# A sparse graph attention kernel: gathers ahead of the edge-to-row matrix, scale and store behind the second square

## The chip, the cores and the metric

The kernel runs on one core of a Trainium2 chip. The metric is the device time in microseconds (us). TensorE is written PE here, VectorE DVE, ScalarE ACT, GpSimd POOL, and SyncE SP.

## What is computed

There are N = 8192 nodes with 128 features. `adj` is an 8192 x 8192 matrix of int32, 256 MB, nearly all zeros (about two ones in a row). The reference, cut to what matters:

```
h = x @ W
e = (h @ a1)[:, None] + (h @ a2)[None, :]
e = where(e > 0, e, 0.2 * e)
e = where(adj > 0, e, -9e15)
attention = softmax(e, axis=1)
z = elu(attention @ h)
y = layernorm(x + z, axis=-1)
```

## The kernel before

It reads all of `adj`, but finds the few ones of each row and works on these alone. A row tile is 128 rows. A step handles two row tiles, so there are 32 steps, numbered 0 to 31 here, and the adj of a step is loaded in four parts of 2 MB, each half the columns of a row tile. Work is spread over a software pipeline: while step n loads and squares, later phases of steps n-1, n-2 and n-3 (in the code p1, p2, p3), and the output of step n-4 (p4), are done. Steps 0 to 5 are written out, 6 to 30 run (in pairs) in a hardware loop with step 30 written out behind it, and step 31, with what is left of the older ones, is a tail in an order of its own. Two places (`g`) alternate for buffers.

In one step, each engine does this, in program order. The order of each engine's queue is what sets the order of the work; there is no planner.

- SP (L353 to L359): four loads of adj, each as soon as a square has freed its slot.
- ACT (L500 to L516): `square_half` 0 to 3 turn the int32 parts into bf16 and count ones (L464). Between them lie `scale` and `store` of p4 (L486 to L498: two activations of 128 x 128 with `shift` and `rstd`, then the output transfer), `distances` of p1 (L475: distance of each edge position to the middle of a row's edges), `copy_sums` of p3 (L482), `exp_weights` of p2 (L467) and `exp_elu` of p3 (L471).
- PE (L640 to L657): `fold_half` 0 (eight products with powers of two, so that eight columns fall into one number), `count_starts` of p1 (a prefix sum of edges, L589), `sum_neighbours` of p3 (L622: gathered rows `nb` times `spread`, 12 instructions of L627 and 4 of L630), fold 1, `send_scores` of p2 (L603, needs the edge-to-row matrix and the gathered rows' scores), `times_W` of p3, `fill_edges` of p1 (L594, sends each edge its row's data), fold 2, fold 3, `send_shares` of p2.
- DVE (L926 to L949): `pick` 0 (L776: eight largest of the folded row and their places), `route` of p1, `neighbour_scores` of p2 (L863, waits for the gathers), pick 1, `rows_to_edges` of p1 (L832), `scores` of p2, `indices` of p1 (L839: copies `edge_in`, then six small operations until `index` at L859), pick 2, `weights` of p2, `finish` of p3 (L903, ends in `mean_var`), pick 3, `edge_weights` of p2 (L896), `lists` of the step itself (L784, ends in `half_len`).
- POOL (L425 to L434): `edges_to_rows` of p1 (L331 to L337: six comparisons that make `edge_row`, the edge-to-row matrix, from `edge_in`), `gather` of p1 (L414: five indirect transfers of 128 rows of x each, from `index`), `norm_factors` of p3 (L401, `rstd` and `shift`), `spread_weights` of p2 (L393, makes `spread`).

`hold` (L50) is a wait with an increment of a spare semaphore. `gather` waits for `index` and for the sum that last read the place it writes. PE's `sum_neighbours` waits for `spread`; fold 1 is behind it in PE's queue; DVE's pick 1 and `rows_to_edges` wait for fold 1; `fill_edges` waits for these; `indices` waits for `fill_edges`.

Of the kernel before, what the change touches and what calls it, by code (L numbers as in the profile page):

```python
# [49 lines left out]
def hold(eng, sem, value, spare):  # L50

    eng.wait_ge(sem, value)
    eng.sem_inc(spare, 1)


def graph_attention(nc, x, adj, W, a, out):
# [39 lines left out]
    with ExitStack() as stack:  # L96
# [213 lines left out]
        def stage(i, g, k):  # L310
            j, place = i - (k - g + 1) // GROUPS, (g - k) % GROUPS
            return None if isinstance(j, int) and not 0 <= j < BODIES else (j, place)
# [18 lines left out]
        def edges_to_rows(eng, j, g):  # L331

            for t in range(PAIR):
                for k, c in enumerate(SPANS[t]):
                    last_one = eng.tensor_scalar(edge_row[:, g, t, k, :], row_iota[:, t * P:(t + 1) * P],  # L335
                                                 edge_in[:, c, ROW_COL:ROW_COL + 1], None, ALU.is_equal)
            last_one.then_inc(edge_row_made, 1)  # L337

        with nc.Block() as block:
# [39 lines left out]
            @block.gpsimd  # L379
            def _(pool):  # L380
                nc.gpsimd.iota(offset[:], pattern=[[1, P]], base=0, channel_multiplier=-1).then_inc(iotas_ready, 1)
                nc.gpsimd.iota(code_base[:].rearrange("p t h s b -> p (t h) s b"),
                               pattern=[[0, PAIR], [-HALF, 2], [0, 8], [-FOLD, BITS]], base=N,
                               channel_multiplier=0).then_inc(iotas_ready, 1)
                nc.gpsimd.iota(row_id[:], pattern=[[P, TILES]], base=1, channel_multiplier=1).then_inc(iotas_ready, 1)
                nc.gpsimd.iota(edge_iota[:], pattern=[[1, EDGES]], base=0, channel_multiplier=0).then_inc(iotas_ready, 1)
                nc.gpsimd.iota(edge_id[:], pattern=[[P, CHUNKS]], base=0, channel_multiplier=1).then_inc(iotas_ready, 1)
                nc.gpsimd.iota(row_iota[:], pattern=[[1, PAIR * P]], base=1, channel_multiplier=0).then_inc(iotas_ready, 1)
                nc.gpsimd.iota(slot_iota[:], pattern=[[1, SLOTS]], base=0, channel_multiplier=0).then_inc(iotas_ready, 1)

                pool.wait_ge(consts_ready, 1)

                def spread_weights(j, g):  # L393
                    hold(pool, edge_w_ready, count(j, g), pool_spare)
                    for t in range(PAIR):
                        mine = edge_w[:, SPANS[t][0]:SPANS[t][0] + SPAN]
                        last = nc.gpsimd.tensor_tensor(spread[:, t, :, :], edge_row[:, g, t, :, :],  # L397
                                                       mine.unsqueeze(2).to_broadcast([P, SPAN, P]), ALU.mult)
                    last.then_inc(spread_ready, 1)

                def norm_factors(j, g):  # L401

                    hold(pool, stats_ready, count(j, g), pool_spare)
                    if not (first(j) and g == 0):
                        hold(pool, scaled, count(j, g) - 1, pool_spare)
                    pool.sem_clear(p_step)
                    v = Steps(pool, p_step)
                    v.after(nc.gpsimd.tensor_tensor(var_eps[:], mean_var[:, :, 1], eps_all[:], ALU.add))
                    v.after(nc.gpsimd.tensor_tensor(rstd[:], var_eps[:], minus_half[:], ALU.pow))  # L409
                    v.after(nc.gpsimd.tensor_tensor(scaled_mean[:], mean_var[:, :, 0], rstd[:], ALU.mult))  # L410
                    nc.gpsimd.tensor_tensor(shift[:], scaled_mean[:], minus_one[:], ALU.mult  # L411
                                            ).then_inc(norm_ready, 1)

                def gather(j, g):  # L414
                    hold(pool, indexed, count(j, g), pool_spare)
                    if not first(j) and not is_final(j, g):
                        hold(pool, summed, count(j, g) - GROUPS, pool_spare)
                    for c in range(CHUNKS):

                        nc.gpsimd.indirect_dma_start(  # L420
                            out=nb_of(j, g)[:, c, :], out_offset=None, in_=x[:, :],
                            in_offset=bass.IndirectOffsetOnAxis(ap=index[:, g, c:c + 1], axis=0),
                            bounds_check=N - 1, oob_is_err=False).then_inc(gathered[g], 16)

                def step(i, g):  # L425
                    p1, p2, p3 = (stage(i, g, k) for k in (1, 2, 3))
                    if p1:
                        hold(pool, edge_in_ready, count(*p1), pool_spare)
                        edges_to_rows(nc.gpsimd, *p1)
                        gather(*p1)  # L430
                    if p3:
                        norm_factors(*p3)
                    if p2:
                        spread_weights(*p2)  # L434

                steps(pool, step)


                gather(*back1)
                spread_weights(*back2)  # L440
                gather(*final)
                norm_factors(*back3)
                spread_weights(*back1)
                norm_factors(*back2)
                spread_weights(*final)
                norm_factors(*back1)
                norm_factors(*final)

            @block.scalar
            def _(act):  # L450
# [3 lines left out]
                def square_half(i, g, q):  # L454
                    h = g * 2 * PAIR + q
                    act.wait_ge(loaded[h % LOAD_SLOTS], i * (16 * HALVES // LOAD_SLOTS)
                                + 16 * (h // LOAD_SLOTS + 1))
                    if not (first(i) and h < SQUARES):
                        act.wait_ge(folded, i * HALVES + (h + 1 - SQUARES))
                    if first(i) and h == SQUARES - 1:  # L460
                        act.wait_ge(s_ready, 1)
                    if q == 0 and not first(i):
                        act.wait_ge(listed, count(i, g) - GROUPS)
                    nc.scalar.activation(square[:, h % SQUARES, :], adj_sb[:, h % LOAD_SLOTS, :], ACT.Square,  # L464
                                         accum_out=half_sum[:, h:h + 1]).then_inc(squared, 1)

                def exp_weights(j, g):  # L467
                    act.wait_ge(scored, count(j, g))
                    nc.scalar.activation(weight[:], score_e[:], ACT.Exp).then_inc(weighed, 1)  # L469
# [12 lines left out]
                def copy_sums(j, g):  # L482
                    act.wait_ge(summed, count(j, g))
                    nc.scalar.copy(x_att[:], x_att_ps[:, :, 0:P]).then_inc(x_att_ready, 1)

                def scale(j, g):  # L486
                    act.wait_ge(norm_ready, count(j, g))
                    if not first(j):
                        act.wait_ge(out_stored[g], j * 16)
                    for t in range(PAIR):  # L490
                        last = nc.scalar.activation(y_out[:, g, t, :], y[:, t, :], ACT.Identity,  # L491
                                                    bias=shift[:, t:t + 1], scale=rstd[:, t:t + 1])
                    last.then_inc(scaled, 1)

                def store(j, g):
                    act.wait_ge(scaled, count(j, g))
                    nc.scalar.dma_start(out_tiles[:, bass.ds(j * BODY + g * PAIR, PAIR), :],
                                        y_out[:, g, :, :]).then_inc(out_stored[g], 16)  # L498

                def step(i, g):  # L500
                    now, p1, p2, p3, p4 = (stage(i, g, k) for k in range(5))
                    square_half(*now, 0)
                    if p4:
                        scale(*p4)
                        store(*p4)
                    square_half(*now, 1)
                    if p1:
                        distances(*p1)
                    if p3:
                        copy_sums(*p3)  # L510
                    square_half(*now, 2)
                    if p2:
                        exp_weights(*p2)
                    if p3:
                        exp_elu(*p3)
                    square_half(*now, 3)  # L516

                steps(act, step)


# [569 lines left out]
```

## Time and profile before

| | |
|---|---|
| median of 3 runs | 827.56 us (827.25 to 828.65) |
| span of the profiled execution | 828.0 us; no other time is listed for it |
| PE busy | 579.1 us, 70% |
| DVE busy | 597.4 us, 72% |
| ACT busy | 548.5 us, 66% |
| POOL busy | 367.6 us, 44% |
| loads of adj and the other transfers of SP's queue | 272.70 MB, 82.5% of 16 DMA engines |
| mean transfer rate | 345 GB/s |

The span is cut into 40 slices on the page, with the busy share of each engine and the rate of the transfers. The table of waits adds up, by pair, who waited for whom. The chain of waits follows the end of the program back to what released each piece of work. The timeline gives start, duration and, in square brackets, the idle time ahead with its releaser. No engine is busy all the time, so the order and the waits matter more than the sums.

### The profile page before, as it was taken

Reading aid. Unit: us, or ns where it says so; the run is one execution under the profiler, and the core shown is the slowest. Engines: PE = TensorE matmul, PEld = TensorE weight load, DVE = VectorE, ACT = ScalarE, POOL = GpSimd, SP = SyncE. Lnnn points to the kernel's source line nnn. Section 1 sums busy time; section 2 is a strip of 40 time slices with the busy share of each in tenths; the row PEclk is TensorE's granted clock in tenths of the full one; section 3 lists DMA queues with packets and bytes.
Section 4 is the critical chain, followed back from the end, with each engine's and each line's share of the span. In section 5 each row is a group of like instructions: output and inputs, shape, how many; then the busy total and the mean of one; then the engine's idle time right before and its main releaser. Section 6 shows DMA issues by size and latency. Waiting matters only on the chain.

```text
span 828.0 us, 11768 instructions
## 1 busy us (share of the span) xinstructions
PE 579.1 (70%) x3037; PEld 400.7 (48%) x3037; DVE 597.4 (72%) x2487; ACT 548.5 (66%) x482; POOL 367.6 (44%) x543
## 2 busy tenths in 40 slices
PE   6965766776766677676666776766677676667764
PEld 6833444554544445444444554544445454444563
DVE  7366677667777877777777777778777777777862
ACT  0586666786676678766766786676678766769311
POOL 0004455444455544444555444455544444555342
PEclk9988689888888998888889888888998888889976
DMA  8999999999999989999999999999999999998000
GB/s 255 428 428 419 420 417 381 362 351 367 369 361 373 399 353 360 372 359 362 357 406 363 363 364 363 361 363 375 385 370 346 378 361 360 359 403 326 19 20 20
DMA packets 34822, 285.57 MB, mean 345 GB/s; under 512 B 5880, under 2 KB 14224, under 8 KB 18416
## 3 DMA queue, kind: packets, MB, share of 16 engines
q1 hardware_dynamic: 20976, 272.70, 82.5%
q0 software_dynamic: 5120, 8.42, 3.0%
q10 hardware_dynamic: 8704, 4.20, 1.7%
q8 instruction: 9, 0.15, 0.1%
q14 instruction: 13, 0.11, 0.0%
HBM read 283.18 MB, written 4.19 MB: 347 GB/s over the span
## 4 chain that ended last, share of the span: by engine, by line
POOL 29%; PE 27%; issue 21%; DVE 11%; DMA 5%; ACT 4%; SPq 2%; POOLq 1%; ACTq 1%; DVEq 0%
POOL nb L420 14%; PE fold L584 10%; PE x_att_ps L627 8%; POOL edge_row L335 8%; PE small L599 5%; DMA adj_sb<-in_adj 4%; ACT square L464 3%; DVE top_map L780 3%; POOL rstd L409 2%; DVE row_edge L835 2%; POOL spread L397 2%; PE x_att_ps L630 2%; DVE top_col L781 2%; SPq L349 1%; DMA nb<-in_x,index 1%
## 5 line engine op out<-in xcount | busy, mean ns | idle before, releaser
L464 ACT ACTIVATE square<-adj_sb 128x4096 bf16<-128x4096 int32 x128 | 462.0, 3611 | 48.1 <-DMA adj_sb<-in_adj 30.1
L584 PE MATMUL fold<-square,bit_ident 128*128 128x512 bf16 x1024 | 268.7, 411 | 84.5 <-ACT square L464 82.5
L335 POOL TENSOR_SCALAR edge_row<-row_iota,edge_in 128x128 f32<-128x128 int32 x180 | 106.3, 604 | 369.5 <-DVE edge_in L845 369.5
L584 PEld LDWEIGHTS fold<-square,bit_ident 128*128 128x128 bf16 x1024 | 100.0, 107 | 221.6 <-ACT square L464 95.9
L420 POOL DMA_INDIRECT nb<-in_x,index x160 | 166.4, 1040 | 61.1 <-issue 43.7
L780 DVE MAX8 top_map<-fold 128x8 f32<-128x512 f32 x128 | 89.3, 697 | 74.8 <-PE fold L584 74.6
L491 ACT ACTIVATE y_out<-y,shift,rstd 128x128 f32<-128x128 f32 x64 | 28.1, 485 | 143.1 <-POOL shift L411 143.1
L627 PE MATMUL x_att_ps<-spread,nb 128*128 128x128 f32 x384 | 98.9, 430 | 5.8 <-POOL spread L397 3.2
L592 PE MATMUL misc<-found,before 128*128 128x2 f32 x64 | 17.9, 349 | 111.7 <-DVE half_len L816 111.7
L627 PEld LDWEIGHTS x_att_ps<-spread,nb 128*128 128x128 f32 x384 | 87.2, 326 | 9.0 <-POOL spread L397 9.0
L781 DVE FIND_INDEX8 top_col<-top_map,fold 128x8 uint32<-128x512 f32 x128 | 88.4, 690 | 0.0
L866 DVE CUSTOM_DVE_ANT_0 dot<-nb,wa_bc 128x128 f32<-128x128 f32 x160 | 37.8, 296 | 57.1 <-DMA nb<-in_x,index 57.1
L592 PEld LDWEIGHTS misc<-found,before 128*128 128x128 f32 x64 | 15.3, 295 | 127.1 <-DVE half_len L816 127.0
L609 PEld LDWEIGHTS misc<-t_slot,edge_row 128*128 128x128 f32 x384 | 51.1, 204 | 16.1 <-issue 12.0
L599 PE MATMUL small<-sent,row_edge 128*128 128x12 f32 (+1 forms) x384 | 45.9, 254 | 17.2 <-DVE row_edge L835 17.2
L609 PE MATMUL misc<-t_slot,edge_row 128*128 128x10 f32 x384 | 48.7, 261 | 11.0 <-DVE t_slot L870 11.0
L397 POOL TENSOR_TENSOR spread<-edge_row,edge_w 128x384 f32<-128x384 f32 x64 | 51.6, 827 | 7.1 <-DVE edge_w L901 7.1
L599 PEld LDWEIGHTS small<-sent,row_edge 128*128 128x128 f32 (+1 forms) x384 | 41.6, 178 | 25.7 <-DVE row_edge L835 24.1
L618 PEld LDWEIGHTS small<-share,row_edge 128*128 128x128 f32 (+1 forms) x384 | 43.1, 176 | 7.3 <-DVE share L892 1.8
L618 PE MATMUL small<-share,row_edge 128*128 128x10 f32 (+1 forms) x384 | 42.0, 242 | 1.2 <-DVE share L892 1.2
L469 ACT ACTIVATE weight<-score_e 128x20 f32<-128x20 f32 x32 | 7.0, 219 | 49.9 <-DVE score_e L884 49.9
L630 PE MATMUL x_att_ps<-empty_diag,x_mean_bc 128*128 128x128 f32 x128 | 39.9, 414 | 0.0
(106 smaller groups left out, 718.9 us busy)
## 6 DMA issues: line engine op xcount, KB each, us to landing
adj_sb<-in_adj SPq DMA_DIRECT2D x128, 2048.0 KB, 9.7
out<-y_out ACTq DMA_DIRECT2D x32, 128.0 KB, 6.1
nb<-in_x,index POOLq DMA_INDIRECT x160, 7.1
W_sb<-in_L_gnn_W SPq DMA_DIRECT2D x1, 64.0 KB, 1.9
x_sb<-in_x SPq DMA_DIRECT2D x4, 0.5 KB, 9.7
a_sb<-in_L_gnn_a SPq DMA_DIRECT2D x2, 0.5 KB, 2.0
```

The source lines that it names most:

```text
L335: last_one = eng.tensor_scalar(edge_row[:, g, t, k, :], row_iota[:, t * P:(t + 1) * P], edge_in[:, c, ROW_COL:ROW_COL + 1], None, ALU.is_e ...
L397: last = nc.gpsimd.tensor_tensor(spread[:, t, :, :], edge_row[:, g, t, :, :], mine.unsqueeze(2).to_broadcast([P, SPAN, P]), ALU.mult)
L420: nc.gpsimd.indirect_dma_start(out=nb_of(j, g)[:, c, :], out_offset=None, in_=x[:, :], in_offset=bass.IndirectOffsetOnAxis(ap=index[:, g, ...
L464: nc.scalar.activation(square[:, h % SQUARES, :], adj_sb[:, h % LOAD_SLOTS, :], ACT.Square, accum_out=half_sum[:, h:h + 1]).then_inc(squar ...
L584: last = nc.tensor.matmul(fold[:, h % LOAD_SLOTS, :], bit_ident[:, b, :], square[:, h % SQUARES, b * FOLD:(b + 1) * FOLD], start=b == 0, s ...
L599: last = nc.tensor.matmul(edge_in_ps[lo:hi, c, :], row_edge[:, g, t, e:e + hi - lo], sent[:, t, :], start=True, stop=True)
L609: last = nc.tensor.matmul(t_row_ps[:, t, :], edge_row[:, g, t, k, :], t_slot[:, c, :], start=k == 0, stop=k == SPAN - 1)
L618: last = nc.tensor.matmul(share_ps[lo:hi, c, :], row_edge[:, g, t, e:e + hi - lo], share[:, t, :], start=True, stop=True)
L627: nc.tensor.matmul(x_att_ps[:, t, 0:P], nb_of(j, g)[:, c, :], spread[:, t, k, :], start=k == 0, stop=False)
L630: last = nc.tensor.matmul(x_att_ps[:, t, 0:P], x_mean_bc[:], empty_diag[:, t, :], start=False, stop=True)
L780: v.after(nc.vector.max(top_map[:, q, :], fold[:, h % LOAD_SLOTS, :]))
L781: nc.vector.max_index(top_col[:, q, :], top_map[:, q, :], fold[:, h % LOAD_SLOTS, :]).then_inc(picked, 1)
```

## The change

POOL issues the gathers of p1 ahead of the comparisons that make its edge-to-row matrix. ACT does scale and store of p4 not between squares 0 and 1, but behind square 1, `distances` and `copy_sums`, ahead of square 2. The tail is unchanged.

```diff
 # POOL
                 def step(i, g):
                     p1, p2, p3 = (stage(i, g, k) for k in (1, 2, 3))
                     if p1:
+                        gather(*p1)
                         hold(pool, edge_in_ready, count(*p1), pool_spare)
                         edges_to_rows(nc.gpsimd, *p1)
-                        gather(*p1)
                     if p3:
                         norm_factors(*p3)
                     if p2:
 # ACT
                     square_half(*now, 0)
-                    if p4:
-                        scale(*p4)
-                        store(*p4)
                     square_half(*now, 1)
                     if p1:
                         distances(*p1)
                     if p3:
                         copy_sums(*p3)
+                    if p4:
+                        scale(*p4)
+                        store(*p4)
                     square_half(*now, 2)
```

## Rows read from the trace of the kernel before

**Rows 1.** The page, part 2: transfer rate in 40 slices of the span.
```profile
GB/s 255 428 428 419 420 417 381 362 351 367 369 361 373 399 353 360 372 359 362 357 406 363 363 364 363 361 363 375 385 370 346 378 361 360 359 403 326 19 20 20
```

**Rows 2.** Table of waits: engine line waited for, us in total, times, longest.
```profile
POOL edge_row L335 <- DVE edge_in L845: 369.5, 30, 59.1
ACT y_out L491 <- POOL shift L411: 143.1, 29, 5.2
...
DVE dot L866 <- DMA nb<-in_x,index: 57.1, 30, 3.1
...
PEld x_att_ps L627 <- POOL spread L397: 9.0, 28, 1.2
```

**Rows 3.** Chain that ended last, in order of time: start, us, engine, tile.
```profile
551.20 1.65 PE x_att_ps L627 x6
...
561.84 1.08 POOL edge_row L335 x2
```

**Rows 4.** Timeline of PE, one step and the start of the next.
```profile
407.85 1.65 PE L627 MATMUL x_att_ps<-spread,nb 128*128 128x128 f32 x6
...
411.75 2.59 PE L584 MATMUL fold<-square,bit_ident 128*128 128x512 bf16 x8
...
416.64 1.38 PE L599 MATMUL small<-sent,row_edge 128*128 128x12 f32 x12 [0.51 <-DVE row_edge L835]
...
425.30 1.90 PE L584 MATMUL fold<-square,bit_ident 128*128 128x512 bf16 x8 [0.59 <-ACT square L464]
431.18 0.59 PE L592 MATMUL misc<-found,before 128*128 128x2 f32 x2 [3.98 <-DVE half_len L816]
431.86 1.65 PE L627 MATMUL x_att_ps<-spread,nb 128*128 128x128 f32 x6
```

**Rows 5.** Timeline of DVE in the same step.
```profile
418.06 0.22 DVE L845 COPY edge_in<-small 128x60 f32<-128x60 f32 x1 [0.54 <-PE small L599]
...
419.35 0.17 DVE L859 TENSOR_SCALAR index<-edge_code 128x5 uint32<-128x5 f32 x1
...
430.43 0.62 DVE L815 TENSOR_SCALAR to_middle<-found 128x2 f32<-128x2 f32 x1
```

**Rows 6.** Timeline of POOL in the same step.
```profile
418.49 3.54 POOL L335 TENSOR_SCALAR edge_row<-row_iota,edge_in 128x128 f32<-128x128 int32 x6 [10.69 <-DVE edge_in L845]
422.20 1.15 POOL L420 DMA_INDIRECT nb<-in_x,index  x1 [0.17 <-issue]
...
427.59 1.04 POOL L420 DMA_INDIRECT nb<-in_x,index  x1 [0.31 <-issue]
...
430.20 1.61 POOL L397 TENSOR_TENSOR spread<-edge_row,edge_w 128x384 f32<-128x384 f32 x2
```

**Rows 7.** Timeline of ACT in the same step.
```profile
407.92 3.62 ACT L464 ACTIVATE square<-adj_sb 128x4096 bf16<-128x4096 int32 x1 [0.68 <-ACT y_out L491]
...
417.56 0.22 ACT L469 ACTIVATE weight<-score_e 128x20 f32<-128x20 f32 x1 [1.16 <-DVE score_e L884]
```

**Rows 8.** Timeline of DVE and of POOL in the tail: last index, first gather behind it.
```profile
789.20 0.21 DVE L845 COPY edge_in<-small 128x60 f32<-128x60 f32 x1
...
790.39 0.17 DVE L859 TENSOR_SCALAR index<-edge_code 128x5 uint32<-128x5 f32 x1
...
791.43 1.08 POOL L420 DMA_INDIRECT nb<-in_x,index  x1 [4.13 <-DVE index L859]
```

**Rows 9.** Timeline of steps 2 and 3, before the hardware loop: DVE, POOL, PE.
```profile
77.95 0.29 DVE L866 CUSTOM_DVE_ANT_0 dot<-nb,wa_bc 128x128 f32<-128x128 f32 x1 [3.14 <-DMA nb<-in_x,index]
...
94.85 1.61 POOL L397 TENSOR_TENSOR spread<-edge_row,edge_w 128x384 f32<-128x384 f32 x2
...
97.72 1.63 PE L627 MATMUL x_att_ps<-spread,nb 128*128 128x128 f32 x6
```

**Rows 10.** Stretches of time (PE, PEld, DVE, ACT, POOL busy; clock; DMA); timeline of PE.
```profile
411.70:413.00 1.30, 1.25 (x3) 0.43 (x4) 0.95 (x9) 1.30 (x4) 0.00 (x0) 0.50 0.73 182
...
816.21 0.83 PE L627 MATMUL x_att_ps<-spread,nb 128*128 128x128 f32 x6
```

## Prediction

> **What bounds the kernel now.** I read the page's transfer rate first. Without stalls the loads of adj move at 428 GB/s, which is 8.39 MB in 19.6 us for one step of two row tiles; later the rate is near 363 [rows 1]. So the transfers could feed a step every 19.6 us, and something else stretches it. From the PE row at 97.72 [rows 9] to the one at 431.86 [rows 4] lie 334.14 us and 14 steps: 23.87 us each.
>
> The table of waits seems to name the culprit: ScalarE waits for `shift` 29 times, 143.1 us, 4.9 us a step, which is the wait that the change goes for. The table also shows GpSimd waiting for `edge_in` (369.5 us), which only says that it sits idle until its part of the step begins, and TensorE's weight load waiting 28 times, 9.0 us in all, for GpSimd's `spread` [rows 2]. That small sum is the important one: TensorE arrives at the neighbour sum only 0.3 us ahead of `spread`, at every step. The chain that ended last says the same: in each step it runs through the neighbour sum on PE (x_att_ps) and edge_row on GpSimd, and not through ScalarE [rows 3].
>
> The loop written out, for one step. `spread` ends at 430.20 + 1.61 = 431.81 and PE starts at 431.86 [rows 4, 6]; one step earlier PE started at 407.85. Its 16 instructions (12 of L627, 4 of L630) take until fold 1 begins at 411.75; fold 1 takes 2.59 (to 414.34); DVE's pick and `row_edge` and PE's `fill_edges` lead to 416.64 + 1.38 = 418.02; DVE copies `edge_in` from 418.06 to 418.28 [rows 4, 5]. GpSimd answers at 418.49, makes the six edge_row pieces (3.54), gathers from 422.20 to 428.63, makes the norm factors until 430.20 and then `spread` (1.61) [rows 6]. The sum is 10.43 + 13.53 + 0.05 = 24.01 us, the whole step. ScalarE is a second loop of nearly the same length: scale, square 1, and fold 1 needs both. Square 1 ends at 407.92 + 3.62 = 411.54, with its accumulator read some 0.1 later [rows 7]; the neighbour sum ends by 411.75. They tie within about 0.1 us. Relieving ScalarE alone can thus gain about 0.1 us a step.
>
> **ScalarE's edit.** Scale (0.88 us), the wait for it and the store's issue come behind `copy_sums`. No work is added. In the present order square 1 starts 1.57 us after scale does (406.35 by the 0.68 and 0.88 ahead of 407.92 [rows 7]); this 1.57 now lies between `copy_sums` and square 2. Today square 2 ends at 417.56 - 1.16 = 416.40, so it starts near 412.7, behind `distances` and `copy_sums`. With squares 0 and 1 out of the way `copy_sums` (0.35 us) can start as soon as the sum ends, about 411.75, and square 2 near 411.75 + 0.35 + 1.57 = 413.7, ending near 417.3. The next instruction behind it, the exponential, isn't released before 417.56 by DVE's `score_e` anyway [rows 7]. That slack swallows the 0.9 us; squares 3 and 0, folds 3 and 0 and DVE's lists keep their places after the sum. DVE's `finish` and GpSimd's norm factors wait for `scaled`, which comes some 8 us earlier than either needs it. The store is one transfer beside loads that have 23.9 - 19.6 = 4.3 us a step to spare. Cost: 0; bounds -0.1 (the tie) and +0.3. The 4.9 us of waiting leave ScalarE, and in their place it waits in `copy_sums` for the sum, behind squares 0 and 1.
>
> **GpSimd's edit.** It takes nothing out of GpSimd's block: five gathers, six edge_row pieces, the factors and `spread` all stay ahead of the end of `spread`. What changes is what the block starts on. Now it starts on `edge_in`, and the 1.24 us until the index is written (418.28 to 419.52 [rows 5]) are hidden under edge_row. Afterwards the block starts on the index:
> - start-to-end, edge_in copy to index takes 1.46 us in the loop, while GpSimd works, and 1.36 in the tail with GpSimd idle (789.20 to 790.56 [rows 8]). I take 1.46 - 0.22 - 0.10 = 1.14 us more.
> - the answer to the release. Edge_row answers `edge_in` in 0.21 us. The gather's 0.17 us behind edge_row [rows 6] is prepared in the shadow of edge_row. Exposed, it is not: in the tail the index ends at 790.56 and the first gather starts at 791.43, 0.87 us [rows 8]. Bounds 0.21 and 0.87; I take 0.87, the same instruction in the same situation.
> - behind the gathers, edge_row starts with a gap of about 0.05.
>
> New head and seams: 1.14 + 0.87 + 0.05 = 2.06; old ones: 0.21 + 0.17 + 0.02 = 0.40. Difference **+1.66 us a step** (bounds +1.0 and +1.8).
>
> What the earlier gathers buy: the first starts at about 420.3 instead of 422.2, so they land 1.8 us earlier, and DVE's wait for them (57.1 us in 30 waits, 1.9 us each [rows 2]) nearly goes. But behind the neighbour products DVE waits again, for fold 1, which is released by `spread`. So this gain is off the loop. edge_row is 2.5 us later; `send_scores` needs it only in the next step. The factors come 1.66 us later, and ScalarE now asks for them two squares later.
>
> **TensorE's clock.** The sum runs at a granted clock of 0.50 (the 1.2 GHz level), and the grant is still 0.50 when fold 1 begins [rows 10]. The stretch from 407.85 to 414.34 (6.49 us) would last 16/6 x 0.83 + 1.90 = 4.1 us wholly at the higher level (six products of the sum in 0.83 us and a fold in 1.90 there) and 3.9 + 8 x 0.42 = 7.3 us wholly at the lower (three fold products in 1.25 us) [rows 4, 10]. The grant is still 0.50 at 413.0, 5.2 us after the sum began. With another period and a longer idle time ahead of the sum the rise may lie elsewhere. The bounds are -2.4 and +0.8 us; today's 6.49 is near the slow end, so a change is likelier to help than to hurt, and I take **-0.3**. That makes +1.36 us a step.
>
> **DVE's lists** now run beside edge_row instead of beside gathers. TensorE's `count_starts` waits for them at 431.18, ahead of the sum [rows 4]. With the sum at 433.2 there are 1.4 us of slack behind `count_starts` (0.6 us). Row: a DVE tensor_scalar beside `spread` takes 0.62 us [rows 5] where its neighbours take 0.17; so a few of DVE's may each lose up to 0.6 us, and one that now loses 0.45 is freed. Cost 0, bounds 0 and +2. The Trainium skill, page "SBUF — State Buffer", section "SBUF: two separate sides", says that the pair of ports shared by the two engines is an exclusive lock, and that DVE operations with two SBUF inputs take part in it as well as those in a 2-port mode. The trace agrees for the tensor_scalar; by the rule in full the time would be that of the third rival, by the rows the 863 below.
>
> **Count and sum.** The loop turns from the sum of step 3 to that of step 30, 27 times. At the start there is a gain: in step 2 DVE waits 3.14 us for the gathers with nothing to cover it [rows 9], and they come 1.8 us sooner; lists then no longer delay the sum of step 3, which follows `spread` (96.46) at once: 96.65 instead of 97.72, -1.1 us. Tail: its order is unchanged and starts on the squares, which keep their distance to the last sum; `spread` of the last looped step has 8 us of slack there. 0 (bounds -1 and +2). Total 828.0 - 1.1 + 27 x 1.36 = **863.6 us**. The span of the profile, 828.0, lies within the three runs (827.25 to 828.65) and 0.4 above their median, and no time around it is listed; I predict 863.
>
> **Rivals.**
> 1. ScalarE's wait for `shift` was the bound. Then the period falls to what the transfers allow, 19.6 us: 828 - 27 x 4.3 = 712 us. For it: the largest wait of a busy engine. Against: rows 3, and the 28 waits of PE for `spread`. A partial form (some 1 us a step, 800 us) would need the gathers' landing to bind. Chance 0.06 together. This is the case on the other side; it decides if TensorE's sum can start earlier than today, which it can't while `spread` is behind the same GpSimd block.
> 2. No change, 828 us: the later index is paid back in full by a clock that rises earlier (1.66 us of the 2.4 possible in each step). 0.03.
> 3. DVE is held up by edge_row so that its lists, not `spread`, release TensorE: 3.5 - 1.4 = 2.1 us more a step, 828 - 1 + 27 x 3.46 = 920 us. It decides from 1.4 us of delay on. For it: the 0.62 us of one operation. Against: the lists hold few operations of that kind. 0.05.
> 4. The gather answers like edge_row, in 0.21 us, and the clock helps a little more: 0.5 us a step, 840 us. 0.08.
>
> My forecast (1.0 to 2.0 us a step, 854 to 881 us) has the other 0.78.
>
> **The numbers.** From the forecast's own 854 to 881, I widen towards rival 4 and for a clock that doesn't help: 845 to 884, which leaves out about 0.19. Faster by over 0.2% (what this kernel's measurement can tell): rival 1, 0.06. Within 0.2%: 0.03. Slower: 0.91.
>
> **What would show it.** Right: a period near 25.2 us; GpSimd's wait ahead of its block goes to the gather, released by DVE's index, and is longer than the 10.7 us of now; the gather begins 0.8 to 0.9 us after the index ends; ScalarE no longer waits for `shift` but for PE in `copy_sums`; PE waits over 1 us for `spread` at each sum; DVE's wait for the gathers is near zero. Wrong: if PE waits for `half_len` directly ahead of the sum (rival 3), if ScalarE waits for transfers (rival 1), or if the first gather follows the index in 0.2 us (rival 4). If the sum's start isn't tied to `spread` in the new profile, the whole argument falls.

## The result and the profile after

The changed kernel takes 875.64 us (median of 4 runs, 874.59 to 878.41) against 827.85 us before (4 runs); ratio 1.059, 95% interval 1.057 to 1.061. It is 48 us slower. The profiled execution took 878.41 us with a span of 876.5.

The page's busy lines and its row of rates:

```profile
PE 595.8 (68%) x2988; PEld 410.5 (47%) x3037; DVE 620.0 (71%) x2487; ACT 549.4 (63%) x482; POOL 372.2 (42%) x543
...
PEclk9977777878788687878868787887877686888975
...
GB/s 266 427 427 422 420 386 370 325 327 323 357 319 387 370 339 316 323 349 319 386 359 318 341 344 336 319 388 356 321 333 328 337 329 389 320 339 333 39 23 19
```

No engine has more work to do (ACT 549.4 us for 548.5, POOL 372.2 for 367.6). The first slices still load at 427 GB/s [rows 1]; the loss starts when the pipeline is full. The granted clock, mostly 8 and 9 tenths before, is 7 and 8.

Table of waits after:

```profile
POOL nb L420 <- DVE index L859: 258.3, 18, 61.2
POOL nb L420 <- issue: 203.3, 138, 13.3
ACT from_middle L478 <- DVE middle L821: 155.6, 30, 7.1
PEld misc L592 <- DVE half_len L816: 152.8, 32, 6.8
...
ACT x_att L484 <- PE x_att_ps L630: 84.6, 32, 7.5
...
PEld x_att_ps L627 <- POOL spread L397: 30.0, 18, 2.7
...
ACT y_out L491 <- POOL shift L411: 7.0, 2, 3.9
```

Against [rows 2]: ScalarE's 143.1 us of waiting for `shift` is 7.0. It has become 155.6 us of waiting for `middle` and 84.6 us for the neighbour sum. The wait wasn't removed but moved, as one expects of an engine that isn't the bound. DVE's wait for the gathers (57.1 us) is gone and gave nothing back. PE waits longer for `spread` (30.0 us for 9.0), but 18 times for 28; in the other steps it waits for DVE's lists.

Two neighbouring steps show both cases. Timeline of PE, then of POOL, after:

```profile
404.19 0.59 PE L592 MATMUL misc<-found,before 128*128 128x2 f32 x2 [5.62 <-DVE half_len L816]
404.64 1.63 PE L627 MATMUL x_att_ps<-spread,nb 128*128 128x128 f32 x6
...
427.48 0.59 PE L592 MATMUL misc<-found,before 128*128 128x2 f32 x2 [3.86 <-DVE half_len L816]
429.95 1.65 PE L627 MATMUL x_att_ps<-spread,nb 128*128 128x128 f32 x6 [1.89 <-POOL spread L397]
```

```profile
402.00 1.62 POOL L397 TENSOR_TENSOR spread<-edge_row,edge_w 128x384 f32<-128x384 f32 x2
416.82 1.15 POOL L420 DMA_INDIRECT nb<-in_x,index  x1 [13.20 <-issue]
...
423.29 3.51 POOL L335 TENSOR_SCALAR edge_row<-row_iota,edge_in 128x128 f32<-128x128 int32 x6
...
428.29 1.61 POOL L397 TENSOR_TENSOR spread<-edge_row,edge_w 128x384 f32<-128x384 f32 x2
```

The sum at 404.64 starts 1.0 us after `spread` is ready (403.62), right behind `count_starts`, which waited for the lists. The sum at 429.95 starts as soon as `spread` ends (429.90). Before, every sum in the loop started on `spread` [rows 4, 6].

For the kernels of this case I took three intervals from the timelines and averaged them over steps 6 to 29. A period is their sum: from the sum's start to the end of `index` (PE, DVE), from there to the end of `spread` (GpSimd's block), and from there to the next sum (a gap that is 0.05 where `spread` releases the sum).

| us per step | sum to index | index to spread | gap | period |
|---|---|---|---|---|
| before | 11.58 | 12.25 | 0.05 | 23.89 |
| after | 10.89 | 14.32 | 0.46 | 25.67 |
| scale only | 11.57 | 12.25 | 0.05 | 23.87 |
| gathers only | 11.15 | 14.25 | 0.26 | 25.66 |
| one piece first | 11.80 | 13.88 | 0.85 | 26.52 |
| three pieces first | 11.33 | 12.76 | 1.32 | 25.40 |
| edge_row last | 11.41 | 10.98 | 2.36 | 24.76 |
| sum first | 11.19 | 14.46 | 0.05 | 25.70 |
| filler in folds | 11.19 | 14.35 | 0.05 | 25.59 |
| edge_row last, sum first | 12.44 | 11.33 | 0.05 | 23.82 |

The mean gap of 0.46 us after the change is made of two kinds of steps: in 10 of the 24 it is 1.0 to 1.1 us, in the other 14 it is 0.05.

From the sum of step 3 to that of step 30 it is 693.9 us after and 644.6 before: 49.3 us. The sum of step 3 is 1.2 us earlier (96.50 for 97.72), the tail 0.4 longer: 48.5, the difference of the spans.

### The profile page after: what moved, and what is told of

It is laid out like the page before. It is cut to its first block, busy times and chain, and to the rows that moved or that the text cites. A ratio compares the mean times of both kernels' runs of the same rounds, so it can differ in the third digit from the quotient of the medians.

```text
span 876.5 us, 11719 instructions
## 1 busy us (share of the span) xinstructions
PE 595.8 (68%) x2988; PEld 410.5 (47%) x3037; DVE 620.0 (71%) x2487; ACT 549.4 (63%) x482; POOL 372.2 (42%) x543
## 4 chain that ended last, share of the span: by engine, by line
PE 28%; DVE 19%; POOL 18%; issue 15%; ACT 11%; DMA 6%; SPq 2%; ACTq 1%; POOLq 1%; another core or an unknown queue 0%; DVEq 0%
PE x_att_ps L627 9%; PE fold L584 9%; ACT square L464 9%; POOL nb L420 7%; POOL edge_row L335 7%; DMA adj_sb<-in_adj 5%; PE small L599 3%; PE x_att_ps L630 3%; PE small L618 2%; POOL spread L397 2%; DVE top_map L780 2%; DVE top_col L781 1%; DVE row_edge L835 1%; POOL rstd L409 1%; DVE empty_diag L899 1%
## 5 line engine op out<-in xcount | busy, mean ns | idle before, releaser
L584 PE MATMUL fold<-square,bit_ident 128*128 128x512 bf16 x978 | 287.2, 444 | 70.7 <-ACT square L464 57.8
L584 PEld LDWEIGHTS fold<-square,bit_ident 128*128 128x128 bf16 x1024 | 109.3, 114 | 212.0 <-ACT square L464 74.2
L478 ACT ACTIVATE from_middle<-edge_iota,middle 128x320 f32<-128x320 int32 x64 | 32.4, 553 | 155.6 <-DVE middle L821 155.6
L335 POOL TENSOR_SCALAR edge_row<-row_iota,edge_in 128x128 f32<-128x128 int32 x180 | 111.3, 630 | 1.3
L484 ACT COPY x_att<-x_att_ps 128x256 f32<-128x256 f32 x32 | 11.9, 372 | 84.6 <-PE x_att_ps L630 84.6
L618 PEld LDWEIGHTS small<-share,row_edge 128*128 128x128 f32 (+1 forms) x384 | 47.3, 188 | 11.0 <-issue 3.9
L618 PE MATMUL small<-share,row_edge 128*128 128x10 f32 (+1 forms) x384 | 44.2, 248 | 1.7 <-DVE share L892 1.7
L630 PE MATMUL x_att_ps<-empty_diag,x_mean_bc 128*128 128x128 f32 x128 | 38.1, 397 | 0.0
```

Source lines behind the costliest of these rows:

```text
L584: last = nc.tensor.matmul(fold[:, h % LOAD_SLOTS, :], bit_ident[:, b, :], square[:, h % SQUARES, b * FOLD:(b + 1) * FOLD], start=b == 0, s ...
L618: last = nc.tensor.matmul(share_ps[lo:hi, c, :], row_edge[:, g, t, e:e + hi - lo], share[:, t, :], start=True, stop=True)
L630: last = nc.tensor.matmul(x_att_ps[:, t, 0:P], x_mean_bc[:], empty_diag[:, t, :], start=False, stop=True)
```

## The experiments

**Each edit alone.** The diffs are the two halves of the change.

> Only GpSimd's edit: gathers ahead of edge_row, ScalarE as before. Theory A (the loop of GpSimd's block, neighbour sum, fold 1, index is the bound, and the block now starts on the index and on a gather whose answer is exposed): ScalarE's wait for shift only moves with the block, so the whole loss is here: 870 to 882 us, period near 25.7 us, gather 1.0 us after the index. Theory B (scale and store behind copy_sums delay square 2 and with it the lists, which makes a good part of the 48 us): this kernel is at 840 to 860 us.

Measured: 877.66 us, ratio 1.059 (1.055 to 1.063), as theory A had it. The same as both edits together, with ScalarE still waiting for `shift`, now longer than the 143.1 us of before:

```profile
ACT y_out L491 <- POOL shift L411: 197.2, 29, 7.9
```

> Only ScalarE's edit: scale and store behind copy_sums, GpSimd as before. Theory A: ScalarE's wait for shift goes, but PE still waits for spread at each sum; 824 to 829 us. Theory B: 835 to 860 us. Theory C (ScalarE's wait was the bound and the gathers' edit hides its gain): below 815 us.

Measured: 827.08 us, ratio 0.999 (0.996 to 1.002). ScalarE's edit alone is worth nothing and costs nothing. The waits are then these:

```profile
PEld misc L592 <- DVE half_len L816: 126.5, 31, 4.8
...
ACT from_middle L478 <- DVE middle L821: 109.2, 31, 5.1
...
ACT x_att L484 <- PE x_att_ps L630: 69.3, 31, 7.2
```

So the whole loss is GpSimd's edit, and the largest wait of a busy engine in the table, 143 us, could be taken away without any effect on the time. Theories B and C fall.

**Hiding the head of the block.** `edges_to_rows` gets a range of pieces, and k of the six go ahead of the gathers:

```diff
-                        gather(*p1)
                         hold(pool, edge_in_ready, count(*p1), pool_spare)
-                        edges_to_rows(nc.gpsimd, *p1)
+                        edges_to_rows(nc.gpsimd, *p1, 0, k)
+                        gather(*p1)
+                        edges_to_rows(nc.gpsimd, *p1, k, 6)
```

> The changed kernel, but GpSimd makes three of the six pieces of edge_row, then the gathers, then the other three. The three pieces (1.8 us) lie under DVE's making of the index and under the answer of the gather. Theory A: the block is as long as before from edge_in on (0.06 us more), so 822 to 834 us. Theory D (early gathers cost by themselves, since edge_row then runs beside DVE's lists and both are slowed): half of it is left, 845 to 860 us.

> The same with one piece of six ahead of the gathers. Theory A: 0.6 us of the exposed head is filled, so the block is 0.6 us shorter than in the changed kernel: 16 us less, 855 to 865 us. If only the order of gathers and edge_row mattered and not what hides the head, it stays at 874 to 878 us.

Measured: k = 3: 862.65 us, ratio 1.042 (1.039 to 1.044); k = 1: 893.08 us, ratio 1.079 (1.075 to 1.083). Both times lie outside every range given. Theory A had the direction of the block, and missed the time. The block did shrink: from index to `spread` 14.32, 13.88, 12.76 for k = 0, 1, 3 (12.25 before), where k = 3 was to cost 0.06 and costs 0.51. The gather's answer isn't the main part of that: it still starts 1.03 us after the index, but the three pieces end 0.79 us after it, so that only 0.24 of it lies bare (0.17 before). Of the 0.51 us, 0.26 lies in the norm factors (1.79 us for 1.53, now beside DVE's lists), 0.08 in the gathers and 0.16 in the rest of the order. Meanwhile the gap between `spread` and the sum went up to 0.85 (k = 1) and 1.32 (k = 3), and with k = 1 the stretch from sum to index grew by 0.9 as well. Something outside the block was late. PE's timeline with k = 3:

```profile
429.13 5.99 PE L588 MATMUL fold<-square,bit_ident 128*128 128x512 bf16 x15 [0.23 <-issue]
...
444.24 0.59 PE L596 MATMUL misc<-found,before 128*128 128x2 f32 x2 [6.27 <-DVE half_len L820]
444.68 1.63 PE L631 MATMUL x_att_ps<-spread,nb 128*128 128x128 f32 x6
```

Folds 2 and 3 together last 5.99 us; a fold at the full clock takes 1.90 [rows 4]. The mean granted clock 10.5 to 16 us after the sum is 1.00 before, 0.72 after and 0.54 with k = 3 (all 24 steps). In the changed kernel it is 0.50 in 13 of them, and all 10 steps with the long gap are among these; in the 10 steps at 1.00 the gap is 0.05. So DVE's picks, and with them its lists, are late, and the lists release `count_starts`, behind which the sum is queued.

**Is it the clock around folds 2 and 3?** The changed kernel with idle products on PE where it waits anyway:

```diff
                         times_W(*p3)
+                        filler(*now, 2, 5)
                     if p1:
                         fill_edges(*p1)
                     fold_half(*now, 2)
+                    if p3:
+                        filler(*now, 3, 12)
```

> The changed kernel with 5 products of 256 columns on PE behind times_W (0.55 us, where PE waits 0.5 us for row_edge) and 12 (1.3 us) between fold 2 and fold 3, where PE waits 1.2 to 1.9 us for square 3; they write into the fold bank that is filled next. Theory K2 (the lists are late in half of the steps since the granted clock falls to the lower level around folds 2 and 3, 10.5 to 16 us after the sum): the grant there goes from 0.75 to near 1.0, the lists begin 18.3 us after the sum and not 18.9, period 25.2 us, 858 to 868 us. Rival (the lists are late by GpSimd's spread and edge_row beside them alone, or the fillers merely delay): 874 to 890 us.

Measured: 872.45 us, ratio 1.054 (1.050 to 1.058), between the two ranges given. What it was to show of the lists came out: the clock in that stretch is 1.00 in every step, the lists begin 18.0 us after the sum (18.9 in the changed kernel, 18.3 before), and the gap is 0.05 us in place of 0.46. Timeline of PE and of POOL there:

```profile
384.67 1.90 PE L584 MATMUL fold<-square,bit_ident 128*128 128x512 bf16 x8
386.41 1.47 PE L644 MATMUL fold<-bit_ident 128*128 128x256 bf16 x12
...
398.10 0.58 PE L592 MATMUL misc<-found,before 128*128 128x2 f32 x2 [3.95 <-DVE half_len L826]
400.62 1.65 PE L627 MATMUL x_att_ps<-spread,nb 128*128 128x128 f32 x6 [1.94 <-POOL spread L397]
```

```profile
387.05 1.14 POOL L420 DMA_INDIRECT nb<-in_x,index  x1 [11.85 <-DVE index L869]
...
393.66 3.78 POOL L335 TENSOR_SCALAR edge_row<-row_iota,edge_in 128x128 f32<-128x128 int32 x6
...
398.95 1.61 POOL L397 TENSOR_TENSOR spread<-edge_row,edge_w 128x384 f32<-128x384 f32 x2
```

Every sum now waits for `spread`, as before the change, and yet only 3 us are won: the stretch from sum to index is 0.3 us longer. All of that is there by the end of fold 1 (6.07 us after the sum for 5.75), where the mean grant 4 to 6.5 us after the sum is 0.82 for 0.90; the fillers ahead of `fill_edges` cost nothing. With the lists out of the way the period is still 25.59. This isolates the main cause: the block of 14.3 us.

**The clock at the sum.** 32 products of 256 columns (3.9 us by the 12 in 1.47 us above) between fold 0 and `count_starts`, in the changed kernel and in the one before:

```diff
                     fold_half(*now, 0)
+                    if p3:
+                        filler(32)
```

> The changed kernel with 32 products of 256 columns (into unused columns of misc) on PE between fold 0 and count_starts, where PE otherwise idles 4 to 6 us, from step 3 on. Theory K (a large part of the step's length is the low granted clock that follows this idle time: the sum takes 3.8 us in place of 2.2, fold 1 and folds 2 and 3 up to 1.7 us longer, which also makes the lists late): sum and fold 1 in 4.1 us, period 23.2 to 24.0 us, 810 to 835 us. Rival (the grant doesn't follow the filler, or the loop is held elsewhere): 870 us or more, since the products then take 6.8 us and delay count_starts.

> The kernel before with the same 32 products. Theory K: the sum takes 2.2 us instead of 3.8, but fold 1 then waits for square 1, which is behind ScalarE's wait for shift and ends 3.7 us after the sum's start; so only fold 1's 0.7 us and some 0.2 us are gained, period 22.9 to 23.2 us, 800 to 812 us. If ScalarE is no second loop: 760 to 775 us.

Measured: in the changed kernel 865.23 us, with runs from 852.35 to 870.24 and no interval; in the one before 822.55 us, ratio 0.995 (0.993 to 0.997). Both stay short of theory K's ranges (810 to 835 and 800 to 812 us), even by their fastest runs (852.35 and 816.79). In the kernel before the clock during the sum (its first 3.8 us) went from 0.50 to 0.93, and sum to index from 11.58 to 10.79 us, but the block grew by 0.10 and the gap to 0.49: the clock then fell in the folds (0.77 at 8.5 to 10.5 us, 1.00 before). A grant held up in one place was lost in another. The other half of the expectation came out: ScalarE binds there. The sum ends 2.14 us after its start (3.78 before), but fold 1 starts 3.67 us after it (3.82 before), since it now waits for square 1. Timeline of PE in the kernel before with the filler:

```profile
303.67 0.94 PE L627 MATMUL x_att_ps<-spread,nb 128*128 128x128 f32 x6 [0.31 <-POOL spread L397]
...
307.80 1.67 PE L584 MATMUL fold<-square,bit_ident 128*128 128x512 bf16 x7 [2.07 <-ACT square L464]
```

By these rows ScalarE's wait for `shift` costs nothing only as long as the sum is slow. In the changed kernel with the filler, where square 1 is done early, fold 1 starts 3.02 us after the sum. ScalarE's edit with this filler and GpSimd's old order is the combination that this suggests, and it wasn't run.

**The sum ahead of count_starts; edge_row last.** In the one edit PE's `sum_neighbours` goes ahead of `count_starts`. In the other, edge_row of p1 follows `spread` of p2, which doesn't need it:

```diff
                         gather(*p1)
-                        hold(pool, edge_in_ready, count(*p1), pool_spare)
-                        edges_to_rows(nc.gpsimd, *p1)
                     if p3:
                         norm_factors(*p3)
                     if p2:
                         spread_weights(*p2)
+                    if p1:
+                        hold(pool, edge_in_ready, count(*p1), pool_spare)
+                        edges_to_rows(nc.gpsimd, *p1)
```

> The changed kernel with GpSimd's order gathers, norm factors, spread, edge_row (edge_row of p1 is read only in the next step). Theory A (the loop runs through GpSimd's block up to spread): the block is 3.6 us shorter, spread is ready 21.6 us after the sum; DVE's lists, ready 23 to 24 us after it, become the bound: period 23.6 to 24.7 us, 820 to 850 us. If instead the early gathers cost by themselves, it stays above 865 us.

> The changed kernel with PE's neighbour sum ahead of count_starts, so that the sum waits for spread alone and not for DVE's lists. Theory A+L (in about half of the steps the late lists, not spread, release the sum, 0.5 us a step): period 25.2 us, 860 to 865 us. Theory A alone (lists only happen to end at the same time, something else holds the loop): 873 to 878 us.

> Both changes of order together: GpSimd gathers, norm factors, spread, edge_row, and PE's neighbour sum ahead of count_starts; ScalarE as in the changed kernel. In the kernel with edge_row last alone, spread was ready 22.4 us after the sum and 2.4 us before the lists let the sum begin. If the sum is let go by spread alone, the period is near 22.4 us, bounded next by DVE (lists, pick 0, route, products, pick 1 against fold 1): 22.4 to 23.3 us, 785 to 810 us. If the lists bind through route and the distances as well (as the kernel with the sum first alone suggests, where nothing was gained), the period stays at 24.4 to 25 us, 838 to 850 us.

Measured: edge_row last 847.57 us, ratio 1.026 (1.023 to 1.029), in theory A's range; sum first 878.75, ratio 1.062 (1.059 to 1.066); both 823.80, ratio 0.994 (0.991 to 0.997). With edge_row last the block is 10.98 us and `spread` is ready 2.36 us too early; the lists bind. This is the intervention on the block itself: 3.3 us shorter brings 28 us although the next bound is only 0.9 us a step away. Timeline of POOL:

```profile
400.75 1.14 POOL L420 DMA_INDIRECT nb<-in_x,index  x1 [10.47 <-issue]
...
408.90 1.61 POOL L397 TENSOR_TENSOR spread<-edge_row,edge_w 128x384 f32<-128x384 f32 x2
410.49 3.56 POOL L335 TENSOR_SCALAR edge_row<-row_iota,edge_in 128x128 f32<-128x128 int32 x6
```

The sum first alone gains nothing: the gap falls by 0.41 us, and that comes back in sum to index (+0.3) and in the block (+0.1). My 860 to 865 us was wrong, and with it the idea that the gap can be won back by itself. Both together, like the filler, beat the kernel before by 4 us with an interval under 1, against the 785 to 810 us hoped for: sum to index is 12.44 us. PE then waits for `t_slot` (46.5 us in all), which is behind `route` in DVE's queue, and `route` behind `count_starts`. The next pair puts DVE's neighbour products ahead of `route`, and makes PE's `send_scores` wait until `route` has read its sums.

> The last kernel (edge_row last, sum ahead of count_starts) with DVE's neighbour products ahead of route (and PE's send_scores waiting for route's reads of the same bank). There PE waited 46.5 us for t_slot, since route waits for count_starts behind the sum, and the products are behind route. If that was its new bound, the period goes from 23.8 to 22.5 to 23.2 us: 785 to 810 us. If lists and clock hold it, 818 to 828 us.

> The same with scale and store between squares 0 and 1, as in the kernel before. Theory A: ScalarE's wait for shift ties with the neighbour sum only as long as the norm factors are made right ahead of spread, which they still are; so the place of scale makes no difference within 0.5%. If ScalarE's edit is worth something once the block is shorter, this one is 5 to 20 us slower than the one with scale behind copy_sums.

Measured: 855.57 us, ratio 1.032 (1.028 to 1.036), and with the old place of scale 804.76 to 826.06 us over four runs, median 822.39, without an interval. The first is far above both ranges. It doesn't test whether `t_slot` was the bound: in its place PE now waits 28.5 us for `route`'s last instruction (`bad`), the wait that came with the edit, and sum to index is 12.75 us. The four runs of the last differ in granted clock and length, so it is no better kernel for certain. With `route` behind the products, `middle` comes later, and ScalarE, whose queue has `distances` ahead of everything up to square 2, waits 207.7 us for it; square 2 starts 8.9 us after the sum in place of 7.7. In the profiled executions the old place of scale, ahead of that wait, is the better one there (square 2 at 7.0 us, period 23.97 for 25.04), where I had expected no difference or the reverse. That the wait in ScalarE's queue makes this difference is argued from these rows and not tried by itself.

## Why the prediction was right

It said 863 us, 845 to 884, slower with 0.91; measured 875.64. The mechanism held: ScalarE alone 0.999, GpSimd alone 1.059, and with the lists kept on time (the filler in the folds) the longer block alone holds the period at 25.59 us. Its terms per step:

- **Head and seams of the block**, forecast +1.66, of which -0.10 for a faster index belongs to the stretch before: so 1.76 from index to `spread`. Measured +2.07. The gather answers 0.98 to 1.06 us after the index, 1.03 on average and not 0.87 as in the tail (+0.16), and edge_row runs a little longer beside DVE's lists (630 ns a piece on the page for 604, +0.13 with its seam). The index that the gather at 416.82 follows, timeline of DVE after:

```profile
415.60 0.17 DVE L859 TENSOR_SCALAR index<-edge_code 128x5 uint32<-128x5 f32 x1
```

The term that I could have left at its lower bound, the answer of 0.21 us, would have been 0.8 off.
- **TensorE's clock**, forecast -0.3. Sum to index went from 11.58 to 10.89, of which 0.04 is the index (1.19 us behind `edge_in` for 1.23, where 0.10 was forecast): -0.65. The direction was right, the size double. Fold 1 took 2.05 us on average for 2.60, and ended 0.67 us earlier after the sum.
- **DVE's lists**, costed at 0 with 1.4 us of slack: wrong, and the step that failed. The measured gap is +0.41 us a step, 11 us in all. I looked for delay by GpSimd alone, and not at what a changed period does to the clock *later* in the step. The grant falls in the folds:

```profile
392.00:395.30 3.30, 3.30 (x8) 1.34 (x9) 2.70 (x11) 3.30 (x1) 2.69 (x3) 0.50 1.00 407
```

(stretch of the changed kernel with fold 3, the columns as in [rows 10]; the clock is 0.50). The filler in the folds shows that this is the cause of the gap. The gap is a term of this sum and not a gain to be had: with it gone (sum first, filler in folds) the period was 25.70 and 25.59 us for 25.67. Delay by GpSimd is there too, but smaller: the lists end 24.18 us after the sum for 23.14, of which 0.60 is their later start and 0.44 their own length. Timeline of DVE after, beside edge_row from 423.29 and `spread` from 402.00:

```profile
402.06 0.81 DVE L809 COPY sent<-code 128x20 f32<-128x20 f32 x1
402.78 0.15 DVE L810 TENSOR_TENSOR expected<-half_sum 128x2 f32<-128x2 f32 x1
402.85 0.81 DVE L813 TENSOR_SCALAR is_code<-code 128x20 f32<-128x20 f32 x1
...
422.63 0.65 DVE L790 TENSOR_TENSOR bit<-top_int,bit_mask 128x256 int32<-128x256 int32 x1
423.20 0.75 DVE L794 TENSOR_TENSOR code_all<-code_base,top_col 128x256 f32<-128x256 int32 x1
```

Before, L809 and L813 took 0.17, L790 and L794 0.42. So operations with two inputs stretch as well, for which the prediction had no row. On this the rule of the Trainium skill, "SBUF — State Buffer", section "SBUF: two separate sides", was the better guide: it puts DVE operations with two SBUF inputs under the shared lock against a GpSimd operation that reads SBUF. The trace agrees only in part: L794 took up to 0.76 us beside edge_row, but in the kernel before L849 and L853, with two inputs of 50 elements, took 0.21 us beside edge_row and 0.21 without it after the change. The price of rival 3 in full (3.5 us a step) didn't come: operations lost 0.2 to 0.6 us each where they met.
- **ScalarE's edit**, costed at 0: 827.08 for 828.24 us.
- **Start and tail**, forecast -1.1 and 0; measured -1.2 and +0.4.

Sum of the terms: +2.07 - 0.69 + 0.41 = 1.79 us, forecast 1.36. The block was 0.31 us worse than forecast and sum to index 0.29 us better. That these two cancel is luck, and what is left of the error, 0.4 us a step or 12 us, is the gap.

Of the signs that the prediction named, the wait ahead of the block (11.0 to 13.5 us a step), its release by the index and DVE's vanished wait for the gathers came. ScalarE waits for PE in `copy_sums`, but more for `middle` ahead of it, which wasn't named. PE waited over 1 us for `spread` ahead of 11 of 24 sums, and 14 of them were tied to it, where the prediction had every one.

Rival 1 (the wait for `shift` as the bound) is refuted by the scale-only kernel, rival 4 (an answer of 0.21 us) by the gather's row; rival 2 by the time. Rival 3 was a part of the truth, in 10 of 24 steps and mainly for another reason than I gave. What stays open: why the answer of the gather is 1.03 us in the loop and 0.87 in the tail, and why the kernel with one piece first is 17 us slower than the changed one, whose block is longer; its sum to index is 0.9 us longer at a lower granted clock (0.75 for 0.90, 4 to 6.5 us after the sum), but what sets that phase wasn't tried.

## What to carry to other kernels

Read the small waits at the join of two engines: "PE for spread, 28 times 0.3 us" named the loop, "ACT for shift, 143 us" a follower of it. A follower can be the next bound: with the sum made fast by the filler, fold 1 waited for ScalarE. In a queue, work that starts on an early signal can hide the making of the later signal and the answer to it; exchange the two and both are laid bare, even if not a single instruction is added. When a period changes, look at TensorE's granted clock over the whole new step and not only where it was low before.

## What the runs showed of the hardware

- An indirect gather answers the release of its wait in 0.98 to 1.06 us in the loop (0.87 in the tail), against 0.21 us for a comparison on the same engine; behind running work ready for it, it follows in 0.17.
- The neighbour sum (16 fp32 products) takes 3.8 us at the 1.2 GHz grant; six of its products 1.65 us there and 0.83 at 2.4 GHz. A fold takes 1.90 us at 2.4 GHz, up to 3.60 at 1.2. Filling TensorE's idle time ahead of the sum raised the grant there from 0.50 to 0.93 and lowered it in the folds behind from 1.00 to 0.77, and the kernel got 4 us faster in all.
- A 20-element copy on DVE takes 0.81 us instead of 0.17 while GpSimd multiplies, an operation with two inputs 0.75 instead of 0.42 while GpSimd compares.
